# Phase stage of a four-part transformer kernel: the third normalisation's statistics as ScalarE running sums

## What is computed

```python
x = x + _L1_attn_ref(_layernorm(x), ...)   # the phase memory
x = x + _L1_ffn_ref(_layernorm(x), ...)    # needs the normalisation of that new x
def _layernorm(x):                          # per token, over its 256 channels
    return (x - mean(x)) / sqrt(var(x) + 1e-5)
```

## Time and profile before

| | |
|---|---|
| median of 3 runs | 4765.62 us (4761.36 to 4766.02) |
| the profiled execution's own time | 4766.11 us |
| its span in the profile | 4764.3 us |
| PE (TensorE matmul) busy | 4519.9 us, 95% |
| DVE (VectorE) busy | 3189.5 us, 67% |
| ACT (ScalarE) busy | 2224.6 us, 47% |
| POOL (GpSimd) busy | 1184.3 us, 25% |
| the phase stage in the trace | from about 2580 to about 3130 us |

### The profile page before, as it was taken

How to read it: one execution, slowest core, us unless ns; L and a number is a source line. 1 busy time by engine, 2 the same in 40 slices (tenths; PEclk the granted TensorE clock), 3 DMA queues, 4 the chain that set the end, 5 groups by cost and what they waited for, 6 DMA issues and landing times. The chain is left out here.

```text
span 4764.3 us, 96779 instructions
## 1 busy us (share of the span) xinstructions
PE 4519.9 (95%) x41096; PEld 3115.7 (65%) x41096; DVE 3189.5 (67%) x3786; ACT 2224.6 (47%) x3664; POOL 1184.3 (25%) x898
## 2 busy tenths in 40 slices
PE   8899999999999998999996999769999999999999
PEld 5433444444333336888884455459999999978888
DVE  7899788888989871463223899836666766644443
ACT  3177777777677673322222566522222222233332
POOL 3522222321312113444441000013323323300000
PEclk9899999999999999999998999879999999999999
DMA  6734544454445325343434356584444444465553
GB/s 186 171 60 79 87 80 72 95 92 75 78 70 97 74 65 154 83 86 76 93 83 118 102 168 168 164 236 103 100 103 85 103 104 101 102 212 176 191 187 107
DMA packets 437421, 545.83 MB, mean 115 GB/s; under 512 B 29296, under 2 KB 361040, under 8 KB 426576
## 3 DMA queue, kind: packets, MB, share of 16 engines
q1 hardware_dynamic: 273616, 414.99, 32.6%
q10 hardware_dynamic: 133120, 67.12, 7.7%
q0 software_dynamic: 30336, 58.74, 6.9%
HBM read 262.63 MB, written 202.60 MB: 98 GB/s over the span
## 5 line engine op out<-in xcount | busy, mean ns | idle before, releaser
L1053 DVE TENSOR_REDUCE att_nmx<-att_s 128x1 f32<-128x1024 f32 x1024 | 1207.1, 1217 | 163.5 <-PE att_s L876 159.4
L1030 ACT ACTIVATE att_pt<-att_sT 128x512 f32<-128x512 f32 x2048 | 1083.4, 604 | 411.3 <-PE att_sT L934 403.7
L876 PE MATMUL att_s<-pick_wide 96*32 96x512 bf16 x5376 | 538.3, 395 | 42.2 <-DVE att_nmx L1053 30.0
L949 PE MATMUL att_o<-att_pt,att_va 128*32 128x512 f32 x4096 | 540.5, 602 | 0.0
L934 PE MATMUL att_sT<-pick_wide 128*32 128x512 bf16 x5376 | 536.7, 383 | 1.5 <-ACT att_pt L1030 0.7
L2809 PE MATMUL sl_lp<-sl_phi,hand_big 128*128 (+1 forms) x4096 | 486.3, 278 | 29.8 <-DMA hand_big<-xnT 20.7
L2798 POOL TENSOR_TENSOR sl_lg<-sl_lg,sl_sm 128x512 f32<-128x512 f32 x256 | 319.6, 1269 | 757.4 <-DVE sl_sm L2949 757.4
L2809 PEld LDWEIGHTS sl_lp<-sl_phi,hand_big 128*128 128x128 f32 x4096 | 473.8, 194 | 36.8 <-issue 36.8
L2873 ACT ACTIVATE sl_lg<-sl_lg 128x1024 f32<-128x1024 f32 x128 | 135.3, 1057 | 765.3 <-DVE sl_lg L2938 765.3
L3056 PE MATMUL cb_op<-hand_big,cb_exT 128*128 128x256 f32 x2048 | 483.8, 379 | 0.0
L2850 PE MATMUL sl_acc<-sl_lg,sl_xn 128*128 128x128 f32 x4096 | 478.2, 275 | 0.8 <-POOL sl_lg L2798 0.8
(11 more groups left out here) (326 smaller groups left out, 6673.2 us busy)
## 6 DMA issues: line engine op xcount, KB each, us to landing
lg<-sl_raw ACTq DMA_DIRECT2D x128, 512.0 KB, 5.7
hand_big<-lg SPq DMA_DIRECT2D x64, 1024.0 KB
qk<-qkv_turned SPq DMA_DIRECT2D x64, 256.0 KB, 3.0
sl_w<-in_L_ffn_W SPq DMA_DIRECT2D x64, 256.0 KB
y<-sl_y SPq DMA_DIRECT2D x16, 1024.0 KB, 6.5
att_qin<-qk SPq DMA_DIRECT2D x62, 256.0 KB, 8.8
pick_wide<-att_hi SPq DMA_DIRECT2D x120, 128.0 KB, 5.1
hand_big<-y SPq DMA_DIRECT2D x7, 2048.0 KB, 8.7
```

The costliest lines, as they stand in the source:

```text
L876: ins = pe.matmul(bank[w * 32:(w + 1) * 32, q, :], QT[n % NB][0:ROWS, h, t * P + w * 32:t * P + (w + 1) * 32], KT[n % NB][0:ROWS, h, q * 5 ...
L949: ins = pe.matmul(o[32 * h:32 * h + 32, :], va[g % 2][:, kt, h, :], pt[:, step % 2, h, c, :], start=kt == 0, stop=kt == NT - 1)
L1030: act.activation(pt[:, step % 2, h, c, :], sT[:, at % 3, :], ACT.Exp, scale=HD ** -0.5).then_inc(exp_done, 1)
L1053: dve.tensor_reduce(nmx[n % 2][:, t, h:h + 1], s[i % 2][:].rearrange("p c k -> p (c k)"), AX.X, ALU.max, negate=True).then_inc(freed, 1)
```

## The change

VectorE's 16 instructions per block (8 bn_stats, 8 bn_aggr) go. ScalarE instead makes 8 Copy activations of `base` into a scratch tile `aside`, each with a running sum per partition (`totals`), then VectorE turns the 8 sums into negative means with one small instruction (`means`, at the place in its queue where `statistics` was), and ScalarE makes 8 Square activations with that negative mean as bias, again with running sums (`spreads`). Both ScalarE parts are queued just ahead of `norm_deviation`, which now takes the sums, scaled by 1/256. Nothing else is moved; no DMA is added or removed.

```diff
+                def totals(p):
+                    act.wait_ge(added, 16 * (p + 1))
+                    if p >= 1:
+                        act.wait_ge(mean_ready, FLOOR + p)
+                        act.wait_ge(var_ready, FLOOR + p)
+                    for t in range(NT):
+                        ins = act.activation(aside[:, t, :], base[p % 2][:, t, :], ACT.Copy, accum_out=total[:, t:t + 1])
+                    ins.then_inc(totalled, 1)
+
+                def spreads(p):
+                    act.wait_ge(mean_ready, FLOOR + p + 1)
+                    for t in range(NT):
+                        ins = act.activation(aside[:, t, :], base[p % 2][:, t, :], ACT.Square, bias=neg_mean[:, t:t + 1],
+                                             accum_out=spread[:, t:t + 1])
+                    ins.then_inc(var_ready, 1)
+
                 def norm_deviation(p):
                     act.wait_ge(var_ready, FLOOR + p + 1)
-                    act.activation(nrstd[:], mv[:, :, 1], ACT.Sqrt, bias=eps[:, 0:1]).then_inc(ndev_ready, 1)
+                    act.activation(nrstd[:], spread[:], ACT.Sqrt, bias=eps[:, 0:1], scale=1.0 / D).then_inc(ndev_ready, 1)
...
                     if old:
+                        totals(p - 2)
+                        spreads(p - 2)
                         norm_deviation(p - 2)
...
-                def statistics(p):
-                    if p >= 1:
-                        dve.wait_ge(var_ready, FLOOR + p)
-                    dve.wait_ge(added, 16 * (p + 1))
-                    for t in range(NT):
-                        ins = dve.bn_stats(stats[:, t, :], base[p % 2][:, t, :])
-                    ins.then_inc(stats_ready, 1)
-                    dve.wait_ge(stats_ready, FLOOR + p + 1)
-                    for t in range(NT):
-                        ins = dve.bn_aggr(mv[:, t, :], stats[:, t, :])
-                    ins.then_inc(var_ready, 1)
+                def means(p):
+                    dve.wait_ge(totalled, FLOOR + p + 1)
+                    if p >= 1:
+                        dve.wait_ge(nmr_ready, FLOOR + p)
+                    dve.tensor_scalar(neg_mean[:], total[:], -1.0 / D, None, ALU.mult).then_inc(mean_ready, 1)
...
-                    dve.scalar_tensor_tensor(nmr[:], mv[:, :, 0], -1.0, nrstd[:], ALU.mult, ALU.mult).then_inc(nmr_ready, 1)
+                    dve.tensor_tensor(nmr[:], neg_mean[:], nrstd[:], ALU.mult).then_inc(nmr_ready, 1)
...
                     if old:
-                        statistics(p - 2)
+                        means(p - 2)
```

More of the change, by code:

```diff
@@ L1995, in phases @@
         base = [st.sb(f"base{j}", [P, NT, D]) for j in range(2)]
-        stats = st.sb("stats", [P, NT, 6])
-        mv = st.sb("mv", [P, NT, 2])
+        total = st.sb("total", [P, NT])
+        spread = st.sb("spread", [P, NT])
+        neg_mean = st.sb("neg_mean", [P, NT])
+        aside = st.sb("aside", [P, NT, D])
         nrstd = st.sb("nrstd", [P, NT])
@@ L2052, in phases @@
         rstd_ready = st.sem("rstd_ready")
-        stats_ready = st.sem("stats_ready")
+        totalled = st.sem("totalled")
+        mean_ready = st.sem("mean_ready")
         var_ready = st.sem("var_ready")
```

## The result

The changed kernel takes 4830.19 us (median of 4 runs, 4828.95 to 4835.72) against 4763.61 us for the kernel before beside it: 66.6 us more, a ratio of 1.0139 (95% interval 1.0127 to 1.0151). The forecast was 4816 with a range of 4798 to 4838, so the sign and the range held, and the size was a quarter short: 50 us forecast, 66.6 measured. The traces place the difference: from kv1 of p = 1 to the first transposes of p = 9 the kernel after takes 495.7 us (2688.43 to 3184.14) and the kernel before 430.8 (2690.03 to 3120.79), 65 us more.

What follows compares the result with a forecast made beforehand. TensorE was taken to bound the steady turns: five at 7.7 us (5.6 stop, 2.1 clock) make 38.5, plus 3.3 for p = 7 and 8.4 for p = 8 and 9, 50.2 us in all: 4816 us, range 4798 to 4838.

Steps and rivals of the forecast that it cites:

- TensorE sets the pace: Phase stage, p = 2 to 6: TensorE bounds the turns, so removing VectorE's 3.30 us a block is worth 0.
- VectorE would have been the bound: Rival, phase stage: VectorE paces the turns, so its relief gives 18.6 us back against 8.4 lost: 4756 us, chance 0.02.
- The price of the sums: ScalarE's path to the square root's table load: Copies 0.416 and Squares 0.486 us each, path 7.6 us longer (6.1 to 10.4).
- the cheap: Rival, ScalarE's sums: accumulator reads hide entirely, path 6.1 us longer; 4794 us, or 4804 with the clock's fall; chance 0.14.
- the dear rival: Rival, ScalarE's sums: reads and activations do not overlap, path 10.4 us longer, 4839 us; chance 0.14 together with table loads.
- The stop of TensorE: Ahead of pv1, p = 2 to 6: TensorE waits 5.6 us a turn for the gelu of gh1.
- p = 7: Turn without gh1: pv1 waits for nobody new, but the second group of transposes comes 3.3 us late.
- p = 8 and 9: Last turns: nothing hides the chain from landed residual to square root, 7.6 us against 3.42; 4.2 us each, 8.4 together.
- The clock: Behind each new TensorE stop, p = 2 to 6: a fall to 1.2 GHz costs 2.1 us (bounds 0 and 2.1).
- the next turn begins from the same relative positions: Steady turns: TensorE cannot catch up, so each turn is 5.6 us longer and the following one starts with unchanged relative positions.

Runs made afterwards that it cites:

- run 2: The kernel before without VectorE's third-normalisation statistics, constants in their place and nothing added: 4746.45 us, ratio 0.9973.
- run 1: The kernel before with VectorE's statistics kept and the sixteen summing activations added to ScalarE at the same queue place, results unused: 4804.43 us, ratio 1.0100.
- Run 6: The changed kernel with its sums moved forward into ScalarE's idle times, and VectorE's means moved ahead of key_values(0): 4762.16 us, ratio 1.0013.
- run 3: The changed kernel with 12 unread fp32 products of 128x512 put into TensorE's stop ahead of pv1: 4818.63 us, ratio 1.0129.
- run 4: The changed kernel with 6 unread fp32 products of 128x512 put into TensorE's stop ahead of pv1: 4802.51 us, ratio 1.0094.
- run 9: The changed kernel with the variance's products woven between those of outB for p = 2 to 7: 4813.35 us, ratio 1.0095.
- run 5: The changed kernel with sums over only 4 of the 8 token tiles: 4769.78 us, ratio 1.0026.
- run 7: The changed kernel with VectorE's means moved behind its two scans: 4817.82 us, ratio 1.0128.
- run 8: The kernel before with the variance's one-column products woven between those of outB for p = 2 to 7: 4745.55 us, ratio 0.9977.

## Why the prediction was right, and where it was short

- **TensorE sets the pace, VectorE's relief is worth nothing in the steady turns**: shown by run 2 (11 us for all of it, from the tail) and by run 1, which has the load of both and stops TensorE for 5.35 us a turn against 5.55. The rule in the Trainium skill (Perfetto Trace Analysis, Identifying the Most-Contended Engine) by which VectorE would have been the bound did not decide here; who waits for whom did.
- **The price of the sums**: 0.40 and 0.49 us apart against 0.42 and 0.49 taken; the path 7.4 to 7.6 us as forecast. Neither the cheap nor the dear rival held. The Trainium skill (ScalarE: Activation LUTs, What ACT_TABLE_LOAD costs) has activations in a row overlap by about 93 ns; with a Copy of 0.41 us an estimate from that alone is 0.32 us from start to start. The trace shows 0.40: the read of 0.19 us takes just that overlap.
- **The stop of TensorE**: forecast 5.6 us five times, measured 5.55. Run 6 shows the mechanism from its other side: with the same work ahead of the slack's limit, there is no stop.
- **p = 7**: forecast 3.3 us, measured 3.1 (pv1's start to `mean`, 17.86 us against 14.74). **p = 8 and 9**: forecast 4.2 each, measured 4.2 from landing to square root. The idle time before the first transposes at p = 8 grew from 17.68 to 21.79 us.
- **The clock**, the step that failed in size: "I charge 2.1 us for each new stop (bounds 0 and 2.1; ...)". It took 4.8: 3.15 at pv1 and 1.65 behind the variance. Two things were missed. The 4.2 us at 1.2 GHz were read off one restart, and taken as the upper bound; another restart takes 6.2. And the turn already had a stretch at 1.2 GHz, so that "the next turn begins from the same relative positions" was wrong for the clock: in the changed kernel this stretch is twice as long. That the turn is longer is not enough for it (run 3: 68.2 us and a short stretch, five times), and what decides between short and long is not shown. 5 x (4.8 - 2.1) = 13.5 of the missing 16 us are this. Another 1.5 are outB of p = 9, 6.74 us in place of 5.23, at the lower clock as well. Together the clock took 24 us in the steady turns, over a third of the whole loss. Runs 3, 4, 1 and 9 each give a part of it back while pv1 starts no earlier against kv1 than in the changed kernel, or 0.2 us earlier (run 1).
- **The range held by luck**: with the clock at its upper bound and the sums as measured, the prediction's own terms end near 4816. 4830 lies in the range because its upper end, 4838, was set by the dear sums, a rival that did not come true.

## What to carry to other kernels

Work moved to an engine with idle time costs by its place in that engine's queue and by how far it exceeds the slack there, not by its length alone: look for the next hand-over behind it and read the slack there (1.96 us here against 7.6 added), then look whether the idle time lies ahead of that place, where the work could go for nothing. If a stop of TensorE of several microseconds comes out of such a sum, the clock can add nearly as much as the stop itself (4.8 against 5.55 us here), and stretches at the lower clock elsewhere in the loop can grow as well. Look at the granted clock of such stretches turn by turn: the same code gave different prices in different turns. Where products of one column stand in a block, weaving them between wider ones is worth a try; it gave 10 us here.

## What the runs showed of the hardware

- A stop of 1.83 us left the product behind it at 2.4 GHz in all five turns (run 5); one of 5.19 to 5.4 us brought it to 1.2 GHz every time (the changed kernel, runs 1, 7 and 9), and the loss on the product behind it was 1.5 to 3.1 us for the same stop in the same kernel (run 1).
- The clock fell not only in stops: 32 records of one column, 3.5 us in which TensorE and its weight loads were busy all the time, were followed by 3.4 us at 1.2 GHz in each steady turn of the kernel before and by 6.8 in each of the changed kernel; in run 5 it was 6.8, 6.8, none, none and 3.4. Woven, eight records at a time, between products of 256 columns they were followed by none (run 8).
- An activation with a running sum is two instructions, and its read of 0.19 us overlaps the activations on either side by about 0.1: with it the start-to-start time is nearly the activation's own duration (0.40 us for one of 0.41, 0.49 for one of 0.49).
- An fp32 product of 512 columns is two records of 0.43 us at 2.4 GHz; a row "x8" of such a product is four matmuls of the program.
